# Six shared PSUM banks in one ring, or four for scores and two for the rest, with the steps of a turn placed anew (attention stage of a Macaron block)

## The reference, cut to what matters

```
x = x + 0.5 * ffn(layernorm(x))
x = x + attn(layernorm(x))          # <- this stage
x = x + 0.5 * ffn(layernorm(x))

def attn(x, wq, w_down, wk_up, wv_up, wo):   # B=16, T=512, E=256, 16 heads of 16
    q = (x @ wq);  lat = x @ w_down
    k = (lat @ wk_up);  v = (lat @ wv_up)
    q, k = rope(q), rope(k)
    scores = einsum('bqhd,bkhd->bhqk', q, k) * 0.25
    allowed = page(key) <= page(query)       # pages of 64 tokens
    p = softmax(where(allowed, scores, min))
    return (einsum('bhqk,bkhd->bqhd', p, v)) @ wo
```

## Time and profile before

| | |
|---|---|
| median of three runs | 2093.88 us |
| the profiled execution | 2093.88 us, span of its instructions 2091.7 us |
| attention stage, first XT to last store issued | about 588 to 1433 us |
| one full turn (b = 1 to 12) | 48.57 us |
| busy in one full turn: PE, DVE, ACT, POOL | 46.1, 35.1, 36.0, 30.4 us |

### The profile page before, as it was taken

The page is one execution under the profiler, slowest core; times in us unless marked ns, Lnnn a source line. Parts: engine busy times, 40 slices in busy tenths (PEclk is TensorE's granted clock), DMA queues, the critical chain, the costliest instruction groups (busy, mean ns, idle before and its releaser), DMA issues. The chain is left out here.

```text
span 2091.7 us, 33769 instructions
## 1 busy us (share of the span) xinstructions
PE 1777.0 (85%) x11330; PEld 1138.1 (54%) x11330; DVE 1242.2 (59%) x3068; ACT 1070.3 (51%) x2132; POOL 884.0 (42%) x948
## 2 busy tenths in 40 slices
PE   5999996999624999999999999996999998876763
PEld 3666665887512454544554444553556665865652
DVE  4878875433215677777777777762877876323221
ACT  4776772111023777777777777774666765100000
POOL 1101101788655555666666666500101100555554
PEclk9999998999856999999999999998999999889997
DMA  2343434999723344333344443312233431767773
GB/s 94 116 147 125 144 129 113 263 261 258 151 90 92 107 124 132 113 113 113 113 128 127 130 124 113 93 42 91 70 108 97 121 119 57 191 162 195 178 174 40
DMA packets 218232, 269.71 MB, mean 129 GB/s; under 512 B 18378, under 2 KB 185322, under 8 KB 218094
## 3 DMA queue, kind: packets, MB, share of 16 engines
q1 hardware_dynamic: 193518, 230.20, 36.3%
q0 software_dynamic: 24576, 37.77, 9.8%
HBM read 136.17 MB, written 80.25 MB: 103 GB/s over the span
## 5 line engine op out<-in xcount | busy, mean ns | idle before, releaser
L1185 DVE TENSOR_REDUCE a_smax<-a_p_ring 128x1 f32<-128x512 f32 (+2 forms) x768 | 354.4, 505 | 171.2 <-PE a_p_ring L1255 166.3
L1094 ACT ACTIVATE a_probs<-a_p_ring 128x512 f32<-128x512 f32 x640 | 363.7, 606 | 101.4 <-PE a_p_ring L1267 99.9
L1255 PE MATMUL a_p_ring<-p_ks,p_qs 100*128 100x512 bf16 (+3 forms) x1024 | 246.5, 305 | 64.2 <-DMA p_ks<-a_parts 30.6
L611 ACT ACTIVATE e_silu<-e_p_up 88x256 f32<-88x256 f32 x128 | 48.7, 380 | 462.1 <-PE e_p_up L653 356.3
L653 PE MATMUL e_p_up<-e_xT,h_w 128*88 128x128 f32 x2048 | 260.4, 283 | 0.0
L47 POOL TENSOR_TENSOR f_rstd<-f_mv,eps 128x4 f32<-128x4 f32 x32 | 25.9, 809 | 550.3 <-DVE f_mv L41 545.7
L1267 PE MATMUL a_p_ring<-p_qs,p_ks 103*128 103x512 bf16 (+3 forms) x1024 | 242.5, 302 | 5.6 <-ACT a_probs L1094 4.4
L653 PEld LDWEIGHTS e_p_up<-e_xT,h_w 128*88 128x88 f32 x2048 | 245.8, 165 | 0.2
L455 PE MATMUL f_p_up<-f_xnT,f_ws1T 128*128 128x512 f32 x384 | 187.2, 610 | 1.5 <-ACT f_xnT L250 1.5
L575 POOL DMA_INDIRECT e_got<-rows,slot_token x128 | 126.5, 988 | 145.9 <-issue 134.7
L625 DVE TENSOR_TENSOR e_hidden<-e_silu,e_p_up 88x256 f32<-88x256 f32 x128 | 53.4, 417 | 223.3 <-ACT e_silu L611 169.7
(11 more groups left out here) (135 smaller groups left out, 3237.0 us busy)
## 6 DMA issues: line engine op xcount, KB each, us to landing
h_w<-w_in SPq DMA_DIRECT2D x128, 352.0 KB
p_qs<-a_parts SPq DMA_DIRECT2D x192, 128.0 KB, 2.5
p_ks<-a_parts SPq DMA_DIRECT2D x192, 128.0 KB, 2.5
h_w<-w_in SPq DMA_DIRECT2D x128, 176.0 KB
rows<-f_row SPq DMA_DIRECT2D x32, 640.0 KB, 6.8
h_x<-x_in SPq DMA_DIRECT2D x16, 512.0 KB, 5.8
acc<-h_x SPq DMA_DIRECT2D x16, 512.0 KB, 2.8
acc<-blank SPq DMA_DIRECT2D x16, 512.0 KB, 4.0
```

Source lines behind the costliest of these rows:

```text
L1094: nc.scalar.activation(to[:], p_score[s][:], ACT.Exp, scale=SCALE).then_inc(score_free[s], 1)
L1185: ins = nc.vector.tensor_reduce(smax[:, t, 4 * g + h:4 * g + h + 1], p_score[s][:, at:at + length], AX.X, ALU.max)
L1255: ins = nc.tensor.matmul(p_score[s][:, at:at + length], qs[1 - u][0:SR + MASK, 4 * g + h, t * P:(t + 1) * P], ks[1 - u][0:SR + MASK, 4 * g ...
```

## The change

The ring is taken apart: four banks (`p_score`) for the `S1` and `S2` steps, two (`p_misc`) for all others, each with its own rotation and semaphores. The tables that place the steps are changed with it. The projections of batch b+2 stand later at their start and closer together, `SUM`, `STATS 0` to `2` are later, `STATS 3`, `NORM` and `MAX 0` a little earlier. No instruction is added or removed: every engine has the same work.

```diff
-RING_BANKS, OUT_BANKS = 6, 2
+SCORE_BANKS, MISC_BANKS, OUT_BANKS = 4, 2, 2
...
-PROJECT = [(0.03, ("XT", 0)), (0.055, ("XT", 1)), (0.09, ("LAT", 0)), (0.13, ("Q", 0)), (0.16, ("SWAP", 0)),
+PROJECT = [(0.07, ("XT", 0)), (0.11, ("XT", 1)), (0.15, ("LAT", 0)), (0.19, ("Q", 0)), (0.21, ("SWAP", 0)),
...
-          + [(0.58, ("NEG", 0)), (0.75, ("MAX", 0))])
+          + [(0.58, ("NEG", 0)), (0.72, ("MAX", 0))])
...
-        p_ring = [ps(f"p_ring{n}", [P, T]) for n in range(RING_BANKS)]
+        p_score = [ps(f"p_score{n}", [P, T]) for n in range(SCORE_BANKS)]
         p_out = [ps(f"p_out{n}", [P, T]) for n in range(OUT_BANKS)]
-        p_score = p_misc = p_ring
+        p_misc = [ps(f"p_misc{n}", [P, T]) for n in range(MISC_BANKS)]
...
-        bank_ready = [sem(f"bank_ready{n}") for n in range(RING_BANKS)]
-        bank_free = [sem(f"bank_free{n}") for n in range(RING_BANKS)]
-        misc_ready = score_ready = bank_ready
-        misc_free = score_free = bank_free
+        misc_ready = [sem(f"misc_ready{n}") for n in range(MISC_BANKS)]
+        misc_free = [sem(f"misc_free{n}") for n in range(MISC_BANKS)]
+        score_ready = [sem(f"score_ready{n}") for n in range(SCORE_BANKS)]
+        score_free = [sem(f"score_free{n}") for n in range(SCORE_BANKS)]
...
-            misc = scores = Rotation(RING_BANKS)
+            misc, scores = Rotation(MISC_BANKS), Rotation(SCORE_BANKS)
```

More of the change, by code:

```diff
@@ L726 @@
 Q_TILES, K_TILES = (0, 2), (1, 3)
-PROJECT = [(0.03, ("XT", 0)), (0.055, ("XT", 1)), (0.09, ("LAT", 0)), (0.13, ("Q", 0)), (0.16, ("SWAP", 0)),
[L728 to L734, removed]
+PROJECT = [(0.07, ("XT", 0)), (0.11, ("XT", 1)), (0.15, ("LAT", 0)), (0.19, ("Q", 0)), (0.21, ("SWAP", 0)),
+           (0.24, ("K", 0)), (0.27, ("SWAP", 1)), (0.32, ("HIGH", 0)), (0.36, ("Q", 1)), (0.38, ("HIGH", 1)),
+           (0.41, ("SPLIT", 0)), (0.44, ("SPLIT", 1)), (0.44, ("K", 1)), (0.45, ("SWAP", 2)), (0.50, ("SWAP", 3)),
+           (0.60, ("HIGH", 2)), (0.68, ("HIGH", 3)), (0.73, ("SPLIT", 2)), (0.76, ("SPLIT", 3))]
+NEXT_INPUT = [(0.47, ("SUM",)), (0.62, ("STATS", 0)), (0.66, ("STATS", 1)), (0.70, ("STATS", 2)), (0.77, ("STATS", 3)),
+              (0.86, ("NORM",))]
+VALUES = [(0.02, ("V", 0)), (0.05, ("V", 1))]
+TAIL = [(0.09, ("OUT", QUADS - 1)), (0.29, ("AT", 0)), (0.33, ("AT", 1)), (0.40, ("WO", 0)), (0.53, ("WO", 1))]
 ALL_MAXIMA = quads_maxima(range(QUADS))
 MAXIMA = ([((n + 0.5) / len(ALL_MAXIMA), step) for n, step in enumerate(ALL_MAXIMA)]
-          + [(0.58, ("NEG", 0)), (0.75, ("MAX", 0))])
-LATE_MAXIMA = [(0.02, ("NEG", 1)), (0.15, ("MAX", 1))]
+          + [(0.58, ("NEG", 0)), (0.72, ("MAX", 0))])
+LATE_MAXIMA = [(0.02, ("NEG", 1)), (0.13, ("MAX", 1))]
 def quads_probs(first, last):
@@ L1271, in turn @@
                             ins.then_inc(score_ready[s], 1)
-                            freed[g, group] = s, (scores.n - 1) // RING_BANKS + 1
+                            freed[g, group] = s, (scores.n - 1) // SCORE_BANKS + 1
                         elif kind == "PV":
```

## The result

The changed kernel takes 2143.42 us (median of 4 runs, 2141.07 to 2155.23), the kernel before 2093.73 in the same session: a ratio of 1.025, 95% interval 1.021 to 1.030, so 50 us slower. The profiled execution took 2149.97 us, span 2147.8, which is 56.1 more than the span before.

What follows compares the result with a forecast made beforehand. A loop of waits through POOL's chain, NORM and PE up to Q 0 sets the 48.57 us turn. Added to 2093.88: 3.1 + 3.4 + 27.6 - 2.3 + 1 = 32.8, so 2126.7, stated as 2126 us; range 2103 to 2148.

Steps and rivals of the forecast that it cites:

- Q 0 later: PE's stretch from the release behind NORM to Q 0's end: 14.30 us in place of 11.65, hidden by nothing.
- From Q 0 to SWAP 0: From Q 0's end on PE to POOL's first SWAP: 1.83 us in place of 2.23, so -0.40.
- POOL's gaps: POOL from SWAP 0 to the scales' end: 31.7 us for 31.98, with about 1.2 of waiting at SPLIT 1.
- MAX 0 earlier: PE waits 2 to 3 us per turn at MAX 0 for POOL's NEG 0; hidden except for the clock.
- The clock: After PE's wait at MAX 0 the clock may halve: +0.5 us a turn if so, 0 if not, taken as 0.3.
- Up to turn 0, and turn 0 itself: Growth ahead of SWAP 0 of turn 0, +3.1 us (bounds 0 and 6), and of turn 0, +3.4.
- After turn 13: After SWAP 0 of turn 13: -2.3 us for Q 0 no longer in front, +1 for dense scores with fewer banks.
- the loop itself: POOL from SWAP 0 to the scales, NORM, PE up to Q 0, back to SWAP 0: 48.57 us, growing to 50.9.
- the signs of being right: SWAP 0 every 50 to 51.5 us, 14.3 to Q 0's end, 2 to 3 at MAX 0, POOL's chain 31 to 32.5.
- Four score banks: Four score banks for six shared: price 0 in the forecast, at most about 1.5 us per turn.
- The rival that gave the banks 1.5 us a turn: Maxima and exponentials hold PE behind MAX 0, NORM up to 1.5 us later a turn: 2147 us; chance 0.12.
- The waits for the ring vanish: Separate rotations remove PE's 1.42 us bank wait at the turn's end; turns fall to 46.92, time 2074; chance 0.07.

Runs made afterwards that it cites:

- e6: The kernel before with Q 0, SWAP 0, K 0 and SWAP 1 at the changed kernel's later places; 2098.80 us, ratio 1.003.
- e5: The kernel before with SUM moved from just ahead of SWAP 2 to just behind it; 2126.57 us, ratio 1.016.
- e4: The kernel before with SUM moved from POOL to DVE at the same place of the list; 2103.54 us, ratio 1.005.
- e1: The kernel before with its own places, only the banks divided into four for scores and two for the rest; 2117.65 us, ratio 1.011.
- e7: The changed kernel with WO 0 at 0.46, behind SWAP 2, instead of 0.40; 2117.57 us, ratio 1.011 to the kernel before.
- e8: The kernel before with SWAP 2 ahead of WO 0, and SUM between SWAP 0 and SWAP 1 on POOL; 2078.35 us, ratio 0.993.
- e10: The kernel before with SWAP 2 ahead of WO 0 and SUM moved from POOL to DVE at 0.30; 2079.78 us, ratio 0.990.
- e2: The kernel before with the new tables of places and the old ring of six banks; 2141.69 us, ratio 1.023.
- e3: The changed kernel with the first seven PROJECT entries (XT 0 to SWAP 1) put back as before; 2150.16 us, ratio 1.027 to the kernel before.
- e9: The changed kernel with MAX 0 put back from 0.72 to 0.75; 2138.29 us, ratio 1.021 to the kernel before.

## Why the prediction was right, and which step of it failed

The direction was right, and the measured 2143 us lies inside the range. The steps one by one:

- *Q 0 later*: predicted 14.30 us from the release to Q 0's end, measured 14.41. *From Q 0 to SWAP 0*: 1.83, measured 1.83 (1002.52 to 1004.35). NORM's 2.71 is 2.71.
- *POOL's gaps*: the wait at SPLIT 1 was put at 1.2 and is 1.30, and the gap at HIGH 1 went. The gap at SWAP 2 was taken to vanish and is 0.31, and 0.21 came at SPLIT 3: the chain is 32.28 for 31.7.
- *MAX 0 earlier*: a wait of 2 to 3 us, measured 2.99. The clock was given 0.3 a turn as a middle between 0 and 0.5; it cost nothing in six turns and 0.5 to 1.65 in six, 6.7 us in all for 3.6.
- *Up to turn 0, and turn 0 itself*: 1.2 and 0.6 us more than predicted. *After turn 13*: +2.0 for -1.3. The 8.0 us outside the stage belong to one execution; the medians differ by 49.7 us for a forecast of 32.

So the period of 50.9 was close to the 51.23 of turn 5. **The step that failed is the loop itself**, in two sentences of the prediction. "Nothing hides it, because PE's stretch is itself a link of the loop": POOL's chain held 1.44 us of gaps ahead of SWAP 2, and these hide the first 1.4 us by which SWAP 0 comes later. e6 shows 0.50 for 2.02. "SUM behind SWAP 2 is the same work in the chain": it had run in the wait for WO 0 and cost nothing, and behind SWAP 2 it costs 2.29 us a turn (e5). The two errors nearly cancel in the sum (a price of 2.25 for Q 0 that is nearly free alone, and 0 for SUM, which costs 2.29). That they do is luck, and the signs of being right did not tell: POOL's chain of 32.28, the 14.41 us to Q 0, the 2.99 at MAX 0 and turns of 51.2 us all came as named, though the loop that they were signs of did not bind.

Read by the loop that binds, turn 5 goes as follows. From PE's release to SWAP 2: 30.02 us before, 967.04 - 936.88 = 30.16 after. From SWAP 2 to the scales' end: 965.11 - 949.27 = 15.84 before, 985.40 - 967.04 = 18.36 after, of which 2.36 are SUM and 0.21 the gap at SPLIT 3. NORM: 2.71 in both. The difference is 0.14 + 2.52 = 2.66, the whole growth from 48.57 to 51.23. A sum around a ring of waits closes on every path that follows the time line, also on one that has slack; that it closed was no evidence. The gap of 0.22 ahead of SWAP 2 was small because SUM filled the wait, and e5 shows the 2.54 that lay beneath it (e4's 3.39 also holds the 0.8 by which DVE's exchange came later).

Two gates explain most of the turns, and the later one sets the turn. Q 0's path needs POOL's 30.54 us without a pause, and then the stretch from the scales to SWAP 0. WO 0's path is the one from the release to SWAP 2, from there to the scales' end, and NORM. In us:

| | by Q 0's path | by WO 0's path | measured |
|---|---|---|---|
| before | 30.54 + 16.59 = 47.13 | 30.02 + 15.84 + 2.71 = 48.57 | 48.57 |
| e1 | 30.54 + 16.80 = 47.34 | 31.01 + 16.18 + 2.71 = 49.90 | 49.90 |
| e5 | 30.54 + 16.58 = 47.12 | 29.99 + 18.16 + 2.71 = 50.86 | 50.86 |
| changed | 30.54 + 18.95 = 49.49 | 30.16 + 18.36 + 2.71 = 51.23 | 51.23 |
| e6 | 30.54 + 18.61 = 49.15 | no gap at SWAP 2 | 49.07 |
| e7 | 30.54 + 18.95 = 49.49 | no gap at SWAP 2 | 49.55 |

Where there is a gap at SWAP 2, the second column is read from the run itself and must close, so it is no evidence by its sum; the evidence is the runs that moved one thing, e5, e6, e7 and e8. The rows leave out a third gate, ACT's cast at SPLIT 3, whose waits lie inside both paths: 0.31 in e1, 0.21 in turn 5 of the changed kernel and 1.87 in its turn 10, 0.30 in e8 and e10, 0.6 to 1.9 in e2 and e3, where the clock fell in every turn.

The changed kernel's Q 0 path is 0.92 us longer than a whole turn before, which is why e7 does not come back to the time before.

*Four score banks* were priced at nothing. With the old places they cost 26 us (e1). With the new places no cost shows (2 us between e2 and the changed kernel, within the intervals), but the two runs differ in more than the banks: PE waits 3.67 us at MAX 0 in e2 for 2.99, and the clock falls in twelve turns for six. Ahead of SWAP 2 the banks still cost 0.38 us a turn (30.16 from the release for 29.78 in turn 5 of e2); e2 loses more than that at SPLIT 3. So the cost seems hidden rather than gone; no run separates it from the clock. The rival that gave the banks 1.5 us a turn had their size about right (1.33 in e1), but their place mostly wrong: 0.34 behind MAX 0, and 0.99 between the release and SWAP 2.

*The waits for the ring vanish*: they did not; PE's wait at the end of the turn is 0.86 for 1.42, for an exponential behind NORM, as the prediction argued.

## What to carry to other kernels

When a loop of waits is closed by adding up a time line, mark each gap on it and start the loop at the last gap before the end: all that stands ahead of a gap has slack, and the loop runs through whoever ended that gap, however small it is. A small gap may hide a long wait that other work fills, so ask for each moved step whether it ran in a wait, and on which side of the gating instruction it lands. Before removing work from an engine, look at what ends its last gap; if it is another engine, the work was free (e4, e10). A sign that both theories predict decides nothing: look for the run in which they differ, as e5 and e6 did.

## What the runs showed of the hardware

**The same wait, two clocks.** PE's wait at MAX 0 was 2.98 to 3.00 us in turns 1 to 12 of the changed kernel; the granted clock stayed at 1.00 (2.4 GHz) in six turns and fell to 0.50 (1.2 GHz) in six. A wait of 3.0 us came with a fall in all twelve turns of e3, one of 0.82 us in turn 6 of e5 only, of twelve such turns, and 1.88 us in turn 0 before. In turn 10, PE's busy time and clock around the wait:

```profile
1234.00:1236.00 2.00, 0.70 (x7) 0.35 (x4) 1.83 (x7) 0.09 (x1) 1.86 (x3) 1.00 1.08 372
1236.00:1238.00 2.00, 0.30 (x4) 0.34 (x4) 0.60 (x2) 1.51 (x3) 1.44 (x6) 0.66 0.96 278
1238.00:1240.00 2.00, 2.00 (x19) 0.60 (x17) 0.00 (x0) 1.09 (x2) 2.00 (x3) 0.50 0.14 47
1240.00:1242.00 2.00, 2.00 (x10) 0.80 (x7) 0.69 (x1) 1.02 (x2) 0.88 (x1) 0.50 0.05 12
1242.00:1244.00 2.00, 2.00 (x12) 0.37 (x10) 1.92 (x8) 1.77 (x4) 1.25 (x2) 0.63 0.00 0
1244.00:1246.00 2.00, 1.78 (x16) 0.89 (x13) 1.87 (x5) 1.73 (x4) 1.46 (x4) 1.00 0.00 0
```

So the length of a wait alone does not tell whether the clock falls. The Trainium skill ("TensorE: Matmul & The Clock Gate", Part 1) has the gate watch PE's activity on a rhythm of its own that does not start with the kernel; these turns agree: in turns 5 to 8 the matmuls ahead of the wait stand within 0.02 us of the same places of the turn, and the clock falls in turns 7 and 8 only.

**What a fall costs depends on where it comes.** In e5 the turn with the fall took 50.88 us for 50.86. In e10 it came behind the release, in the stretch up to Q 0, and the turn took 49.38 for 47.74.

**The last expert stage varies by 19 us with the same code**, and the clock with it. Its length, busy PE, and clock in e9 and in e10:

```profile
1485.88:2131.70 645.82, 509.62 (x2976) 365.48 (x2977) 339.14 (x838) 244.91 (x497) 199.56 (x192) 0.95 0.48 127
```

```profile
1425.50:2090.20 664.70, 533.36 (x2976) 392.72 (x2977) 337.47 (x838) 244.69 (x497) 200.02 (x192) 0.91 0.47 124
```

Where a stage is changed, its own length in the trace is sharper than the span: the attention stage of e9 and that of the changed kernel differ by 1.6 us (893.92 and 895.56), and their spans differ by 16.1 us.

**DVE and POOL lengthen each other.** In e10 SUM on DVE took 2.14 us while POOL computed (the median of 15), for 1.50 in e4, where POOL stood idle for most of it, and POOL's addition beside it 2.07 for 1.27. That such a delay decided a turn is not shown:

```profile
935.46 2.14 DVE L1197 TENSOR_TENSOR a_x<-a_x,a_x_odd 128x1024 f32<-128x1024 f32 x1
```

```profile
936.66 2.07 POOL L1052 TENSOR_TENSOR a_qk<-a_qk,a_swapped 128x512 f32<-128x512 f32 x1
```
